# Bias of a fused feed-forward: written into PSUM by ScalarE in place of a bias product on TensorE

## The reference, cut to what matters

```
x = x + L0_xattn(layernorm(x), ctx)          # attention, 32 heads of 128
x = x + L0_ffn(layernorm(x))                 # the stage of the change
x = x + L1_xattn(layernorm(x), ctx)
x = x + L1_ffn(layernorm(x))

L0_ffn:  Xd = quant_dequant_fp8(X)           # rows in chunks of 128
         D  = gelu(Xd @ W0d.T + bias0)       # 512 -> 1792
         Dd = quant_dequant_fp8(D)
         E  = Dd @ W1d.T + bias1             # 1792 -> 512
```

## Time and profile before

| | |
|---|---|
| median of three runs | 1663.48 us |
| span of the profiled execution, first to last instruction | 1663.4 us (no other time of this execution is given) |
| mean granted TensorE clock | 0.968 of full speed |
| TensorE matmul busy | 1510.4 us, 91% |
| VectorE busy | 1273.3 us, 77% |
| ScalarE busy | 789.3 us, 47% |
| GpSimd busy | 289.0 us, 17% |
| feed-forward 0, first to last product | 1027.2 to 1378.6 us of the span |

### The profile page before, as it was taken

One profiled execution on the slowest core, in us unless ns is written; L12 is line 12 of the kernel. 1 busy time (PEld: TensorE's weight loads), 2 busy tenths in 40 slices (PEclk: granted clock), 3 DMA queues, 4 the chain that ended last, 5 costly groups with the idle time before them and its releaser, 6 DMA issues. The chain is left out here.

```text
span 1663.4 us, 29998 instructions
## 1 busy us (share of the span) xinstructions
PE 1510.4 (91%) x11382; PEld 803.7 (48%) x11398; DVE 1273.3 (77%) x2386; ACT 789.3 (47%) x1677; POOL 289.0 (17%) x249
## 2 busy tenths in 40 slices
PE   5799999999999999999999987799999998787695
PEld 4455455555555555555555543344444544344353
DVE  6577667667677667767776786899999986999777
ACT  3343433424334243342333332566777763888652
POOL 2001002001011011011011001111211103789620
PEclk7799999999999999999999998899999999899898
DMA  7031231321312212221312112122222350767402
GB/s 265 1 78 51 68 85 26 79 75 43 98 39 66 76 52 64 68 61 52 77 51 62 48 70 102 23 45 45 45 44 44 58 117 1 140 107 123 79 1 101
DMA packets 273838, 113.48 MB, mean 68 GB/s; under 512 B 239154, under 2 KB 255539, under 8 KB 273460
## 3 DMA queue, kind: packets, MB, share of 16 engines
q1 hardware_dynamic: 234820, 78.67, 21.6%
q10 hardware_dynamic: 38896, 33.03, 6.3%
HBM read 44.57 MB, written 11.53 MB: 34 GB/s over the span
## 5 line engine op out<-in xcount | busy, mean ns | idle before, releaser
L627 PE MATMUL xp<-WO,OT 128*128 128x512 f16 x1536 | 341.1, 382 | 5.6 <-DVE X L824 5.6
L585 PE MATMUL pj<-XT,WQ 128*128 128x512 f16 x1536 | 339.0, 381 | 6.4 <-PEq L379 6.4
L627 PEld LDWEIGHTS xp<-WO,OT 128*128 128x128 f16 x1536 | 148.2, 98 | 189.3 <-issue 18.4
L585 PEld LDWEIGHTS pj<-XT,WQ 128*128 128x128 f16 x1536 | 148.4, 98 | 182.3 <-DVE WKV L294 6.7
L705 ACT ACTIVATE E<-E 128x512 f32<-128x512 f32 x64 | 40.1, 627 | 329.0 <-DVE E L801 329.0
L824 DVE SCALAR_TENSOR_TENSOR X<-xp,X 128x512 f32<-128x512 f32 x128 | 88.2, 690 | 113.0 <-PE xp L627 112.0
L565 POOL TENSOR_TENSOR VW<-VW,XB 128x1024 f32<-128x1024 f32 x14 | 32.9, 2351 | 769.8 <-DVE VW L107 769.8
L1028 PE MATMUL db<-W0T,XD 128*128 128x448 f16 x768 | 162.2, 363 | 0.0
L1045 PE MATMUL eb<-W1T,DT 128*128 128x512 f16 x672 | 147.7, 380 | 4.2 <-ACT EB L1120 2.5
L766 DVE SCALAR_TENSOR_TENSOR QT<-pj,QT 128x512 f16<-128x512 f32 x128 | 88.0, 687 | 67.9 <-ACT QT L688 67.6
L1028 PEld LDWEIGHTS db<-W0T,XD 128*128 128x128 f16 x768 | 76.9, 100 | 74.7 <-issue 8.0
(11 more groups left out here) (236 smaller groups left out, 2427.0 us busy)
## 6 DMA issues: line engine op xcount, KB each, us to landing
W0T<-in_L_xattn_wq ACTq DMA_DIRECT2D x7, 1024.0 KB, 5.3
W0T<-in_L_xattn_wo ACTq DMA_DIRECT2D x7, 1024.0 KB, 5.0
CS<-in_ctx SPq DMA_DIRECT2D x4, 1024.0 KB, 10.1
X<-in_x SPq DMA_DIRECT2D x4, 1024.0 KB, 11.2
out<-X SPq DMA_DIRECT2D x8, 512.0 KB, 3.6
XB<-in_L_ffn_W ACTq DMA_DIRECT2D x28, 128.0 KB, 2.8
w0t<-XB ACTq DMA_DIRECT2D x7, 512.0 KB, 3.3
w1t<-W0T ACTq DMA_DIRECT2D x7, 512.0 KB, 3.8
```

The costliest lines, as they stand in the source:

```text
L585: last = pe.matmul(bank[:, :], w, src[:, b, k, tokens], start=n == 0, stop=n == 3 * KC - 1)
L627: last = pe.matmul(xp[i % 2][:, :], OT[:, a, j, i * P:(i + 1) * P], WO[:, b, j, :], start=n == 0, stop=n == 3 * REP - 1)
```

## The change

From the second tile on, ScalarE writes the scaled bias into each PSUM bank once its reader has emptied it, and TensorE's products accumulate onto it, without a bias product. The first tile keeps its five bias products, which also open the accumulation in the banks. New on ScalarE: `seed_e(older)` behind `x_times_rec`; `seed_d` of quarters 0 and 1 behind gelu 2, of quarters 2 and 3 behind gelu 3, ahead of `high_x`. For this both biases are loaded into all 128 partitions. The scaled copies go, with VectorE's scaling and two memsets on GpSimd; `ones` has 64 in its first row. TensorE's waits for gelu_done and eb_done become waits for d_seeded and e_seeded.

```diff
-        B0, B1, B0S = SH[0:1, 0:INNER], SH[0:1, INNER:INNER + DIM], SH[:, INNER + DIM:2 * INNER + DIM]
-        B1S = sb(ph, "B1S", [P, DIM], BF16)
+        B0, B1 = SH[:, 0:INNER], SH[:, INNER:INNER + DIM]
...
-            sp.dma_start(B0[:, :], b0.partition_broadcast(1)).then_inc(S["b_ld"], 16)
-            sp.dma_start(B1[:, :], b1.partition_broadcast(1)).then_inc(S["b_ld"], 16)
+            sp.dma_start(B0[:, :], b0.partition_broadcast(P)).then_inc(S["b_ld"], 16)
+            sp.dma_start(B1[:, :], b1.partition_broadcast(P)).then_inc(S["b_ld"], 16)
...
                     if live(ahead(i, -1)):
-                        pe.wait_ge(S["gelu_done"], count(i, 4, q - 3))
-                    pe.matmul(db[q][:, 0:NQ], ones[:, :], B0S[:, q * NQ:(q + 1) * NQ], start=True, stop=False)
+                        pe.wait_ge(S["d_seeded"], count(i, 4, q - 3))
+                    else:
+                        pe.matmul(db[q][:, 0:NQ], ones[:, :], B0[:, q * NQ:(q + 1) * NQ], start=True, stop=False)
...
                 if live(ahead(i, -1)):
-                    pe.wait_ge(S["eb_done"], count(i, 1, 0))
-                pe.matmul(eb[:, :], ones[:, :], B1S[:, :], start=True, stop=False)
+                    pe.wait_ge(S["e_seeded"], count(i, 1, 0))
+                else:
+                    pe.matmul(eb[:, :], ones[:, :], B1[:, :], start=True, stop=False)
...
-                    pe.wait_ge(S["bias_ready"], 2)
+                    pe.wait_ge(S["b_ld"], 32)
...
+            def seed_d(i, qs):
+
+                for q in qs:
+                    if fixed(i) == 0 and q == 0:
+                        act.wait_ge(S["b_ld"], 32)
+                    act.wait_ge(S["gelu_done"], count(i, 4, q + 1))
+                    act.activation(db[q][:, 0:NQ], B0[:, q * NQ:(q + 1) * NQ], ACT.Copy, scale=WEIGHT_SCALE).then_inc(S["d_seeded"], 1)
...
+            def seed_e(i):
+                act.wait_ge(S["eb_done"], count(i, 1, 1))
+                act.activation(eb[:, :], B1[:, :], ACT.Copy, scale=WEIGHT_SCALE).then_inc(S["e_seeded"], 1)
...
                     x_times_rec(after)
+                if live(older) and live(ahead(older, 1)):
+                    seed_e(older)
                 if live(i):
                     gelu(i, (0, 1, 2))
+                    if live(nxt):
+                        seed_d(i, (0, 1))
...
                 if live(i):
                     gelu(i, (3,))
+                if live(i) and live(nxt):
+                    seed_d(i, (2, 3))
                 if live(nxt) and fixed(i) != -1:
                     high_x(nxt)
...
-            for zeros in (B0S, B1S):
-                pool.memset(zeros[:, :], 0.0).then_inc(S["bias_zeroed"], 1)
             pool.memset(ones[:, :], 0.0).then_inc(S["ones_done"], 1)
             pool.wait_ge(S["ones_done"], 1)
-            pool.memset(ones[0:1, :], 1.0).then_inc(S["ones_done"], 1)
+            pool.memset(ones[0:1, :], WEIGHT_SCALE).then_inc(S["ones_done"], 1)
```

More of the change, by code:

```diff
@@ L954, in ffn0 @@
         names = ("w1_ld b_ld kvw_hi kvw_lo qw_hi "
-                 "xt_done xt_hi xt_lo d_done ones_done bias_zeroed bias_ready gelu_done da_done dstep dw_done dcut dbits dm_done dsum "
+                 "xt_done xt_hi xt_lo d_done ones_done gelu_done d_seeded e_seeded da_done dstep dw_done dcut dbits dm_done dsum "
                  "dq_done dqs_done dh_done dl_done dt_done e_done eb_done x_done")
@@ L1024, in first_product @@
                     if live(ahead(i, -1)):
-                        pe.wait_ge(S["gelu_done"], count(i, 4, q - 3))
-                    pe.matmul(db[q][:, 0:NQ], ones[:, :], B0S[:, q * NQ:(q + 1) * NQ], start=True, stop=False)
+                        pe.wait_ge(S["d_seeded"], count(i, 4, q - 3))
+                    else:
+                        pe.matmul(db[q][:, 0:NQ], ones[:, :], B0[:, q * NQ:(q + 1) * NQ], start=True, stop=False)
                     for n, (k, (a, b)) in enumerate([(k, ab) for ab in PASSES for k in range(KC)]):
                         last = pe.matmul(db[q][:, 0:NQ], XD[:, i[1] % 2, a, k, :], W0T[:, b, k, q * NQ:(q + 1) * NQ],
-                                         start=False, stop=n == 3 * KC - 1)
+                                         start=False, stop=n == 3 * KC - 1, skip_group_check=live(ahead(i, -1)))
                     last.then_inc(S["d_done"], 1)
@@ L1045, in second_product @@
                         last = pe.matmul(eb[:, :], DT[:, a, c, :], W1T[:, b, c, :],
-                                         start=False, stop=c == IC - 1 and (a, b) == PASSES[-1])
+                                         start=False, stop=c == IC - 1 and (a, b) == PASSES[-1], skip_group_check=live(ahead(i, -1)))
                 last.then_inc(S["e_done"], 1)
@@ L1164, in step @@
                     act.wait_ge(loaded1["sq_ld"], 16)
+                    act.wait_ge(S["e_seeded"], TILES - 1)
                     for j in range(REP):
@@ L1220, in low_keys_values @@
                     low_kv1(dve, db[unit], unit // 2, unit % 2)
[L1222 to L1226, removed]
             def step(i):
@@ L1231, in step @@
                     low_x(nxt)
-                    scale_biases()
                 if live(hidden):
```

## The result

The changed kernel takes 1674.05 us (median of four runs, 1672.72 to 1677.93) against 1663.46 us: a ratio of 1.0062, 95% interval [1.0048, 1.0076]. That is 10.6 us slower where 4.35 us was forecast, and above the forecast range. The direction was right, and so was the mechanism in the middle of the stage; the start and the end cost more than I had given them.

A forecast was written before the change was run, and what follows sets the result against it. The prediction took a VectorE and ScalarE loop of 19.49 us a tile as the bound, with TensorE at 19.55 us. Seeds 4.0, start 0.6, end -0.7 and +0.45 gave +4.35 us: 1667.8 us, range 1662.5 to 1671.5.

The forecast's parts named there:

- What bounds the stage: Middle of the stage: VectorE and ScalarE loop at 19.49 us a tile; TensorE, at 19.55, falls 0.06 us behind.
- Part 1: Bias products from the second tile: of 14.6 us TensorE work removed, only 0.06 us a tile in eight tiles could show.
- Part 2: Seeds on ScalarE: those of quarters 2 and 3 ahead of high_x cost 0.27 us a tile, 4.0 us in all.
- 2s - 0.61: Cost a tile of two seeds of s us each, less 0.61 us taken up ahead of d_times_rec: 0.27 us.
- Part 3: TensorE's new waits for the seeds, with any fall of the clock in them, cost nothing.
- the same slack: TensorE's 1.2 us a tile in hand, taken to pay for clock falls in its waits.
- Part 4: Start of the stage: first product waits for both bias loads and starts at 1027.8, 0.6 us late.
- Part 5: End of the stage: 0.70 us comes back ahead of the last amax; last second_product's wait for its seed costs +0.45 us.
- The case "+8.65": Whole stage: seeds at 0.53 us each and a late bias load, or an often falling clock: 1672.1 us, chance 0.10.

The follow-up runs named there:

- e1: Kernel before without bias products from the second tile on and without any seed, so output lacks biases there: 1664.16 against 1665.31 us, ratio 0.9993.
- e2: Changed kernel with bias products kept in all but the last second_product, overwriting the seeds: 1673.58 us, ratio 1.0053.
- e7: Changed kernel with seeds moved, first tile's biases by rows, last second_product opened by a bias product, 12 spare products ahead of it: 1665.96 against 1665.67 us.
- e3: Changed kernel with seed 2 moved up behind gelu 2 and seed 3 moved behind high_x: 1668.17 us, ratio 1.0020.
- e5: Changed kernel with the last second_product alone opened by a bias product again, without its seed: +10.2 us, ratio 1.0071.
- e12: Same program as e5 (changed kernel, last second_product opened by a bias product), measured in another session: 1680.05 us in one run.
- e11: Changed kernel measured again with nothing altered: 1673.19 us in one run.

## Why the prediction was wrong, point by point

- **What bounds the stage.** Right. TensorE's period was the longer by 0.06 us, but what it fell behind by showed only at the end: e1 took 0.98 us a tile off TensorE and got 0.79 us there, e2 put the seeds on ScalarE and got the whole longer period.
- **Part 1, the bias products, worth next to nothing.** Right (e1, e7).
- **Part 2, the seeds.** The mechanism was right and proved by e3. The size was low: 0.44 us a seed was taken from the gelu's row and 0.47 us was measured, so the difference 2s - 0.61 came out at 0.33 us, not 0.27, and the term at 4.7 us in fourteen tiles and 0.4 in the first, 5.1 us, not 4.0. Where the price is a small difference of large numbers, 7% of an instruction is 25% of the term. The Trainium skill (ScalarE: Activation LUTs, What ACT_TABLE_LOAD costs) led to 0.47 us, and the trace agrees. Its sentence that ScalarE reaches PSUM faster than SBUF (Step-by-step: what each stage is for) didn't show: two seeds stand 0.47 us apart, two gelus, which read PSUM and write SBUF, 0.43, and a seed of 512 columns and the output of eb take 0.58 us alike.
- **Part 3, "it is paid from the same slack; I cost it at nothing".** This step failed. Through the middle it held. But at the last second_product there is no slack: TensorE waited 3.77 us, where it had waited 2.51, and the clock fell to 0.77 in the window; +2.5 us. The seed is not needed for it: e1 has none, and 1.7 us of it. I had written of a wait of 2.33 us with a fallen clock in the same part, and didn't look for the one place where such a wait stands on the path. e5 and e12 add that behind a wait of 3.15 us the price isn't paid in every run. The Trainium skill (TensorE: Matmul & The Clock Gate, What's actually happening) has the clock released by activity and throttled by default; the rows agree, without telling which wait is long enough.
- **Part 4, the start.** The wait was right and mis-sized, the largest miss. Both loads together were to land 4.05 us behind the first issue, as one load of 576 KB. The first product started 6.91 us behind it in the profile, and 5.5 to 6.6 us in the other six kernels with this load in its way. Against the first low_x it came 3.35 us later than before (2.0 us in e11), not 0.6, and later than the high end of my range, 2.1 us. The large load is not what failed: its 448 KB were there in 3.4 us, and the same interpolation gives 3.7 for them. What failed is the overlap: I let the last 128 KB land as soon as the bytes ahead of them were through, and put W1T's load behind both. They took 6.3 us from their own issue, 4.8 to 5.9 in the other six, where the row of that size has 2.8. Why stays open. Bytes of W1T moved beside them, but no run leaves W1T's load away from behind the biases, so neither its share nor that of the larger load ahead is shown.
- **Part 5, the end.** -0.78 us for -0.7, and the seed +0.41 us for +0.45: right, but for the clock. The 0.1 us for the engine to see its own end shows in no run: the seed starts 0.03 us behind it.
- **Sum.** Forecast 4.0 + 0.6 - 0.7 + 0.45 = 4.35. Measured in the stage, in the same order: 5.14 + 3.73 - 0.78 + 2.92 = 11.0 (3.73 is the load with the clock's later rise, 2.92 the seed and the fallen clock). The forecast had the sign right; two terms carry the miss, the load (+3.1) and the fallen clock (+2.5). The case "+8.65" came nearest, but not for its reasons: a seed cost 0.47 us, not 0.53, and of the two falls of the clock at the stage's end only one cost time.

What stays open is the fate of the clock in waits of 2 to 3.2 us, and the spread of whole times outside the stage. The windows 1500 to 1600 us of the changed kernel and of e12, whose program there is the same though the windows cut it a little differently, show granted clocks of 0.91 and 0.86:

```profile
1500.00:1600.00 100.00, 70.77 (x832) 37.61 (x833) 83.50 (x152) 75.23 (x152) 75.84 (x76) 0.91 0.56 90
```

```profile
1500.00:1600.00 100.00, 72.23 (x873) 38.02 (x872) 83.18 (x141) 73.35 (x151) 78.11 (x78) 0.86 0.55 93
```

## What to carry to other kernels

An engine that is busy 19.95 of 20 us need not be the bound: compare the periods of all engines, and if one chain that never waits for the busy engine is as long, work taken off the busy engine buys nothing and work put into that chain costs its full length. Moved work is priced by its place: two seeds ahead of high_x cost 0.34 us a tile, and with one of them in the idle time before and the other behind high_x the same four cost 0.03. And look where a stage begins and ends, since a late load or a cooled clock that the middle hides is paid there in full.

## What the runs showed of the hardware

- A load of 448 KB over 128 partitions landed 3.3 to 3.8 us behind its issue, and one of 128 KB, issued 0.4 us behind it and 0.5 us ahead of one of 3.5 MB, 4.8 to 6.3 us behind its own (ten traces); loads of 128 KB elsewhere in the kernel have a median of 2.8 us.
- Ahead of the last two groups of 42 products, TensorE's clock fell in all six waits of 3.77 us or more. Behind 3.15 us it fell in one of two executions of one program, behind 2.38 us in three of four. It fell also behind 2.09, 2.39 and 2.71 us, and not behind 2.41 to 2.59 us (five waits). The price was 1.7 to 2.7 us on the 42 products.
- An ACTIVATE of 448 columns from SBUF into PSUM starts 0.47 us behind its like, one from PSUM into SBUF 0.43 us.
- VectorE's two off_grid_d instructions (128x896, fp32) took 3.16 us with GpSimd at a subtraction beside them, 2.93 us with GpSimd at the shorter scaling alone, and 2.09 us in the stage's last tiles, with GpSimd idle.
